# Second cross attention's first rows loaded by GpSimd, first experts' weights loaded a stage ahead

## The reference

```python
x = x + L0_attn(layernorm(x))                      # attention with a sigmoid/tanh/relu score
x = x + L0_xattn(layernorm(x), ctx, ctx)           # cross attention, 8 heads of 128
x = x + L0_ffn(layernorm(x))                       # 8 experts, top 2, width 1024
x = x + L1_attn(layernorm(x))
x = x + L1_xattn(layernorm(x), ctx, ctx, mask)     # cross attention, 16 heads of 16, below
x = x + L1_ffn(layernorm(x))                       # 64 experts, the best one
```

```python
# L0_ffn: routing, then the experts
logits = einsum('bsh,eh->bse', x, gate_w) + expert_bias
top_w, top_i = top_k(softmax(logits), 2)
for e in range(8):
    h = gelu(einsum('bsh,ih->bsi', x, w_up[e]), approximate=False)
    out += sparse_w[..., e:e + 1] * einsum('bsi,hi->bsh', h, w_down[e])
# L1_xattn
q, k, v = x @ Wq, ctx @ Wk, ctx @ Wv               # split into 16 heads of 16
A = softmax(q k^T / 4 - mask * 1e9)
x + (A v) @ Wo
```

## Time and profile before

| | |
|---|---|
| median of 3 runs | 2875.01 us (2874.33 to 2880.67) |
| profiled execution | 2879.26 us |
| its span | 2877.5 us |
| TensorE busy | 2514.8 us (87%) |
| VectorE busy | 2087.2 us (73%) |
| ScalarE busy | 1446.5 us (50%) |
| GpSimd busy | 1059.3 us (37%) |
| moved by DMA | 266.68 MB, mean 93 GB/s |

### The profile page before, as it was taken

One profiled execution on the slowest core, in us unless ns is written; L12 is line 12 of the kernel. 1 busy time (PEld: TensorE's weight loads), 2 busy tenths in 40 slices (PEclk: granted clock), 3 DMA queues, 4 the chain that ended last, 5 costly groups with the idle time before them and its releaser, 6 DMA issues. The chain is left out here.

```text
span 2877.5 us, 59452 instructions
## 1 busy us (share of the span) xinstructions
PE 2514.8 (87%) x19717; PEld 2098.5 (73%) x19717; DVE 2087.2 (73%) x4615; ACT 1446.5 (50%) x3401; POOL 1059.3 (37%) x1584
## 2 busy tenths in 40 slices
PE   7987899999758999999499999999996979996582
PEld 5875788888757999999378888888885956664231
DVE  5884898998637777776488888888875567774664
ACT  3542334334235777777265555655552456663041
POOL 3331545445301111110265555555532014333366
PEclk9988999999978999999699999999998989997586
DMA  8012000000176666664200000000002733230845
GB/s 310 0 32 88 1 1 0 0 0 0 31 292 249 220 220 220 220 219 156 90 14 10 16 7 15 7 15 9 7 1 65 246 102 87 81 88 11 267 142 168
DMA packets 156638, 266.68 MB, mean 93 GB/s; under 512 B 20944, under 2 KB 130464, under 8 KB 143200
## 3 DMA queue, kind: packets, MB, share of 16 engines
q1 hardware_dynamic: 140400, 215.91, 22.1%
q0 software_dynamic: 11168, 31.21, 3.7%
q10 hardware_dynamic: 4944, 17.96, 1.6%
HBM read 191.85 MB, written 73.17 MB: 92 GB/s over the span
## 5 line engine op out<-in xcount | busy, mean ns | idle before, releaser
L1723 ACT ACTIVATE a_prob<-a_s_ps,a_ntop 128x256 f32<-128x256 f32 x512 | 235.6, 473 | 304.3 <-DVE a_ntop L1808 304.3
L1776 POOL TENSOR_TENSOR a_prob<-a_prob,a_rden 128x1024 f32<-128x1024 f32 x128 | 242.5, 1895 | 302.4 <-DVE a_rden L1813 302.4
L3204 POOL DMA_INDIRECT e0x_xg<-token_rows,e_order x78 | 75.3, 965 | 384.7 <-PE e0x_t_ps L3251 342.5
L2411 ACT ACTIVATE x1a_prob<-x1a_st_ps,x1a_mask_now 128x512 f32<-128x512 f32 x256 | 162.2, 686 | 92.0 <-PE x1a_st_ps L2330 90.6
L1301 ACT ACTIVATE x0b_sq<-x0b_f 128x1024 f32<-128x1024 f32 x64 | 67.9, 1060 | 274.2 <-DVE x0b_f L1375 274.1
L2486 DVE TENSOR_REDUCE x1a_top<-x1a_s_ps 128x4 f32<-128x1024 f32 x128 | 154.9, 1222 | 66.9 <-PE x1a_s_ps L2314 65.0
L1808 DVE TENSOR_REDUCE a_ntop<-a_s_ps 128x4 f32<-128x1024 f32 x128 | 156.2, 1221 | 38.9 <-PE a_s_ps L1646 38.8
L68 PE MATMUL e0x_up_ps<-e0x_xT_high,e0x_up_w_high 128*128 128x256 f32 x624 | 180.4, 289 | 1.1 <-DVE e0x_up_w_low L3331 1.1
L68 PE MATMUL e0x_up_ps<-e0x_xT_high,e0x_up_w_low 128*128 128x256 f32 x624 | 177.5, 285 | 0.0
L68 PE MATMUL e0x_up_ps<-e0x_xT_low,e0x_up_w_high 128*128 128x256 f32 x624 | 177.3, 284 | 0.0
L68 PE MATMUL e0x_y_ps<-e0x_down_w_high,e0x_hT_high 128*128 128x256 f32 x624 | 176.6, 283 | 0.0
(11 more groups left out here) (648 smaller groups left out, 8708.1 us busy)
## 6 DMA issues: line engine op xcount, KB each, us to landing
e0x_up_raw<-up_rows SPq DMA_DIRECT2D x39, 1024.0 KB, 4.8
e0x_down_raw<-down_rows SPq DMA_DIRECT2D x39, 1024.0 KB
x_qk<-head_rows SPq DMA_DIRECT2D x384, 64.0 KB
head_rows<-x1p_rows_out SPq DMA_DIRECT2D x32, 512.0 KB, 3.8
e1w_ew<-in_L_ffn_expert_w_dram SPq DMA_DIRECT2D x8, 2048.0 KB
sorted_tokens<-zeros SPq DMA_DIRECT2D x10, 1024.0 KB, 19.6
sorted_results<-e0x_y SPq DMA_DIRECT2D x39, 256.0 KB
down_rows<-e0w_downT ACTq DMA_DIRECT2D x8, 1024.0 KB, 7.3
```

The costliest lines, as they stand in the source:

```text
L1723: last = act.activation(prob[:, h % RING, n, t, :], s_ps[:, n, t * SEQ:(t + 1) * SEQ], ACT.Exp, bias=ntop[:, h % RING, n, t:t + 1], accum_ ...
L1776: last = pool.tensor_tensor(p, p, scale_of, ALU.mult)
L2411: last = act.activation(prob[:, c % 2, j, 2 * (h % 2):2 * (h % 2) + 2, :], st_ps[:, :, j * SEQ:(j + 1) * SEQ], ACT.Exp, bias=mask_now[:, p ...
```

## The change

Two parts. In the first, a new class `Ahead` places the gate's weights and the first two copies of up and down matrices in SBUF at addresses that in the first cross attention belong to the context and the start of `wg` (so `wg` now comes before `out_bias`), and an SP block in `l0_cross_batches` loads them once the last F product is done. They have semaphores of their own, and the loads at the routing stage's start go. In the second, the 56 loads of batches 0 and 1 of the second cross attention are issued by GpSimd in the projections' block, as soon as that batch's stores are there, on semaphores `s_first`; SP issues from batch 2 on, and TensorE waits for `s_first` in batches 0 and 1.

```diff
-        self.out_bias = sb(cross, "x0_out_bias", [P, DIM])
         self.wg = [cross.enter_context(nc.sbuf_tensor(f"early_x0_wg_{part}", [P, KC, INNER], F32R)) for part in ("high", "low")]
+        self.out_bias = sb(cross, "x0_out_bias", [P, DIM])
...
         with nc.Block() as block:
+
+            @block.sync
+            def _(sp):
+                sp.wait_ge(filled["F"], COUNT["F"] * BATCH)
+                ahead.load(sp)
...
+        s_first = [[sem(f"rows{p}{half}_first") for half in range(2)] for p in range(2)]
...
+        def load(engine, b, p, half, landed):
+            i0 = slice(half * HALF, (half + 1) * HALF)
+            for n in range(2):
+                for side in range(2):
+                    for r, name in enumerate(ROWS_OF[side]):
+                        at = 64 * n + XROWS * r
+                        engine.dma_start(qk[p][at:at + XROWS, side, i0, :].bitcast(F32),
+                                         by_pair[PLANE[name], n][:, bass.ds(PAIRS * b + half * HALF, HALF), :]).then_inc(landed[p][half], 16)
+                at = 64 * n + 3 * XROWS
+                engine.dma_start(qk[p][at:at + 2, 1, i0, :].bitcast(F32),
+                                 head_rows.mask[:, bass.ds(b, 1), :].broadcast_to([2, HALF, SEQ])).then_inc(landed[p][half], 16)
...
                 pool.wait_ge(s_fixed, 7)
+                pool.wait_ge(s_rows, 32)
+                for b in range(2):
+                    pool.wait_ge(s_stored[b], 16 * KC)
+                    for half in range(2):
+                        load(pool, b, b, half, s_first)
...
-                for b in range(2):
-                    for half in range(2):
-                        load(b, b, half)
-
                 def batch(b, p):
                     for half in range(2):
                         sp.wait_ge(s_st, PAIRS * b + HALF * (half + 1))
-                        load(b + 2, p, half)
+                        load(sp, b + 2, p, half, s_ld)
...
                     if h % HALF == 0:
-                        pe.wait_ge(s_ld[p][h // HALF], 16 * LOADS * (turn + 1))
+                        if isinstance(turn, int) and turn == 0:
+                            pe.wait_ge(s_first[p][h // HALF], 16 * LOADS)
+                        else:
+                            pe.wait_ge(s_ld[p][h // HALF], 16 * LOADS * turn)
...
-                if given is None:
+                if given is None and ahead is None:
                     sp.dma_start(gw[:], gate_w).then_inc(s_w, 16)
                     sp.dma_start(gb[:], broadcast_row(gate_b)).then_inc(s_w, 16)
...
-                    pe.wait_ge(s_w, 32)
+                    pe.wait_ge(ahead.s_gate if ahead else s_w, 32)
...
             if n % 2 == 0:
-                pe.wait_ge(self.loaded[e % self.COPIES][n // 2], 16 * (e // self.COPIES + 1))
+                if self.first and e < self.COPIES:
+                    pe.wait_ge(self.first[e][n // 2], 16)
+                else:
+                    pe.wait_ge(self.loaded[e % self.COPIES][n // 2], 16 * (e // self.COPIES + (0 if self.first else 1)))
...
     def load(self, sp):
         first = TurnedWeights.COPIES
-        self.up.load(sp, 0, first)
-        self.down.load(sp, 0, first)
         self.up.load(sp, first)
         self.down.load(sp, first)
...
+class Ahead:
...
+    def load(self, sp):
+        sp.dma_start(self.gw[:], self.gate_w).then_inc(self.s_gate, 16)
+        sp.dma_start(self.gb[:], broadcast_row(self.gate_b)).then_inc(self.s_gate, 16)
+        self.up.load_ahead(sp, self.s_up)
+        self.down.load_ahead(sp, self.s_down)
```

More of the change, by code:

```diff
@@ L158, in __init__ @@
         self.c_rstd = sb(cross, "c_rstd", [P, TILES])
+        self.wg = [cross.enter_context(nc.sbuf_tensor(f"early_x0_wg_{part}", [P, KC, INNER], F32R)) for part in ("high", "low")]
         self.out_bias = sb(cross, "x0_out_bias", [P, DIM])
-        self.wg = [cross.enter_context(nc.sbuf_tensor(f"early_x0_wg_{part}", [P, KC, INNER], F32R)) for part in ("high", "low")]
         self.c1 = sb(cross, "x0_c1", [P, XH])
@@ L653, with l0_cross_attention @@
 INNER = XH * HD
-def l0_cross_attention(nc, sh, early, weights, w1, b1, g1, be1, w2, b2, w_up, up_rows):
+def l0_cross_attention(nc, sh, early, weights, w1, b1, g1, be1, w2, b2, w_up, up_rows, ahead):
     with ExitStack() as ctx:
@@ L2202, in _, with l1_cross_attend @@
                 over_batches(dve, batch)
-def l1_cross_attend(nc, sh, head_rows, gate, wo, v, sel, mask_col, qk, top_rows):
+def l1_cross_attend(nc, sh, head_rows, gate, wo, v, sel, mask_col, qk, top_rows, s_ld, s_first, load):
     HALF = PAIRS // 2
@@ L2560, in doubling_sum, with route @@
     return a
-def route(nc, sh, name, experts, top_k, tiles, gate_w, gate_b, slots, weights, table, chosen, beside=None, beside_out=None, beside_rows=None, load=None, granule=P, given=None, rows=None, found=None):
+def route(nc, sh, name, experts, top_k, tiles, gate_w, gate_b, slots, weights, table, chosen, beside=None, beside_out=None, beside_rows=None, load=None, granule=P, given=None, rows=None, found=None, ahead=None):
     E, K = experts, top_k
@@ L2571, in route @@
         sb, ps, sem = alloc(nc, ctx, name)
-        gw = sb("gw", [E, DIM])
+        gw, gb = (ahead.gw, ahead.gb) if ahead else (sb("gw", [E, DIM]), sb("gb", [P, E]))
         gwT = sb("gwT", [P, KC, E])
-        gb = sb("gb", [P, E])
         XN = 2 if rows is None else 4
@@ L2886, in __init__ @@
         self.experts = w.shape[0]
+        self.first = None
     def allocate(self, ps, sem):
@@ L2897, in signals, with load_ahead @@
         self.filled, self.drained = sem(f"{self.name}_in_psum"), sem(f"{self.name}_turned")
+    def load_ahead(self, sp, first):
+        self.first = first
+        for e in range(self.COPIES):
+            for half in range(2):
+                sp.dma_start(*self.half_of(e, half)).then_inc(first[e][half], 16)
     def load(self, sp, first=0, end=None):
@@ L3027, in dispatch_programs, with __init__, keep @@
     return vector, pool
+class Ahead:
+    TABLES = 248
+    def __init__(self, nc, sh, ctx, gate_w, gate_b, w_up, w_down):
+        E, I = w_up.shape[0], w_up.shape[1]
+        sem = lambda name: ctx.enter_context(nc.semaphore(f"ahead_{name}"))
+        self.gate_w, self.gate_b = gate_w, gate_b
+        self.s_gate = sem("gate_loaded")
+        self.s_up = [[sem(f"up{e}_half{half}_loaded") for half in range(2)] for e in range(TurnedWeights.COPIES)]
+        self.s_down = [[sem(f"down{e}_half{half}_loaded") for half in range(2)] for e in range(TurnedWeights.COPIES)]
+        with ExitStack() as space:
+            sb = lambda name, shape: space.enter_context(nc.sbuf_tensor(f"ahead_{name}", shape, F32))
+            sb("tables", [P, self.TABLES])
+            up_nat = sb("up_nat", [P, TurnedUp.COPIES, I // P, DIM])
+            down_nat = sb("down_nat", [P, TurnedDown.COPIES, KC, I])
+            self.gw = sb("gw", [E, DIM])
+            self.gb = sb("gb", [P, E])
+        self.words = TurnedUp.COPIES * I // P * DIM + TurnedDown.COPIES * KC * I + DIM + E
+        self.up = TurnedUp(sh, "up", w_up[AHEAD:E], up_nat, 2)
+        self.down = TurnedDown(sh, "down0", w_down[0:AHEAD], down_nat, 2)
+    def load(self, sp):
[3 more added lines that the diff above has]
+        self.down.load_ahead(sp, self.s_down)
+    def keep(self, nc, ctx):
+        ctx.enter_context(nc.sbuf_tensor("ahead_kept", [P, self.words], F32))
 class ExpertRows:
@@ L3052, in l0_experts @@
     with ExitStack() as ctx:
+        ahead.keep(nc, ctx)
         sb, ps, sem = alloc(nc, ctx, "e0w")
@@ L3060, in l0_experts @@
         down.signals(sem)
[L3061 to L3068, removed]
+        halves = TurnedHalves(ahead.up, ahead.down, rows_of.up[AHEAD * P:E * P, :], rows_of.down[0:AHEAD * P, :])
+        route(nc, sh, "e0r", E, K, NP, None, None, slots, weights, table, None, halves, (upT, downT[0]), (s_rows,),
+              load=lambda sp: down.load(sp, 0, TurnedDown.COPIES), granule=GROUP, rows=scratch.rows, ahead=ahead)
         with ExitStack() as invert:
```

33 lines of the change are left out of this document (12 added, 21 removed).

## The result

The changed kernel takes 2868.86 us at the median of 17 runs, the kernel before 2874.87 in 17 runs beside it: a ratio of 0.9976, 95% interval [0.9965, 0.9987]. So it is faster by about 0.24%: some 7 us by the ratio, 6.0 between the medians. The forecast was 27 us; 2868.86 lies above the top of its range. The profiled execution took 2867.18 us, 1.7 under its median, where that of before was 4.25 over the median of its first three runs.

A forecast was written before the change was run, and what follows sets the result against it. It took DMA waits in the routing stage and at the seam before the second cross attention as the bounds. Gains of 21 + 6 = 27 us gave 2852.3 profiled, 2848 for the median; range 2841 to 2862.

The forecast's parts named there:

- The gate's 2.9 us: Routing stage's start: TensorE begins with the block instead of waiting for the gate's weights, saving 2.9 us.
- The third pair, 12.2 us: Routing stage: the third pair, 17.21 us against the second's 4.98, gets its up weights earlier, saving 12.2 us.
- step (c): Routing stage's last pair: with 4.2 of 23 MB gone, less stands in front of its load, saving 7.4 us.
- I take 21, near the upper end: Routing stage: total gain taken as 21 us, between 13 and 22.5, since stores catch up while no load runs.
- The lower bound: Routing stage: loads at 105 GB/s throughout, up and down experts each 4.7 us late, leaving a gain of 13 us.
- rival 1: Routing stage stays bound by DMA: gain 13 + 6 = 19 us, time 2856; chance 0.17.
- The seam, 8.2 us: Between projections and second cross attention: first score 7.5 us sooner, 0.7 of the second wait; 8.2 together, at most 9.5.
- GpSimd's 56 issues in 30 us: Projections: GpSimd issues the 56 row loads in 30 us by the direct row, 53 by the indirect one.
- Rival 5: Slower: GpSimd's issues so slow that the attention waits for rows; at 2.5 us each, 12 slower, 2887; chance 0.04.
- The price in the projections, 2 us: Projections: row loads exceed the spare DMA room and delay context loads, costing 2 us of the seam's gain.
- rival 2: The projections pay the whole gain of the seam: gain 21 + 0, time 2854; chance 0.10.
- rival 4: Ahead loads land late or something else holds the pairs: only the seam's 6 us left, 2869; chance 0.03.

The follow-up runs named there:

- ahead_only: The changed kernel with the 56 row loads back on SP at the attention's start, weights still loaded ahead: 2865.14 us, ratio 0.9965 to the kernel before.
- stores_end: The changed kernel with all eight stores of turned expert weights issued behind the routing stage's last pair: 2856.89 us, ratio 0.9925 to the kernel before.
- pool_only: The kernel before with only the row loads issued by GpSimd, weights loaded as before: 2876.21 us, ratio 1.0003 to the kernel before.
- stores_late: The changed kernel with each routing-stage store of turned expert weights issued three pairs later: 2861.3 us, ratio 0.9954 to the kernel before.
- all_paced: The changed kernel with GpSimd's 56 row loads issued four at a time behind each of 14 stored batches: 2862.63 us, ratio 0.995 to the kernel before.
- first_paced: The changed kernel with GpSimd loading batch 0 alone, two loads behind each stored batch, SP loading batch 1 at the attention's start: 2860.11 us, ratio 0.9943.
- first_unpaced: The changed kernel with GpSimd loading batch 0 alone, 28 loads in one burst, SP loading batch 1 at the attention's start: 2871.91 us, a single run.
- e0r_t_ps: Not a run: a buffer in the routing stage that TensorE's matmuls write from ident and e0r_xn; no time of its own.
- e0r_xn: Not a run: the tile of VectorE's normalising in the routing stage, whose first operation marks the stage's start; no time of its own.
- e0r_up_ps: Not a run: a buffer in the routing stage that TensorE's matmuls write from ident and ahead_up_nat; no time of its own.

## Why the prediction was wrong

The direction was right (faster had 0.92), the size wasn't: 27 us were forecast, about 7 came. Step by step:

- **The loads ahead cost nothing**: right. They were issued from 735.56 to 741.9 and done by 750, in the empty stretch.
- **The gate's 2.9 us**: right. The stretch with that wait is 3.0 shorter.
- **The third pair, 12.2 us**: right to 0.1 by itself (17.21 to 4.98), but the fourth pair went from 4.99 to 12.24. **The last pair, 7.4**: in the change's profile 6.5 came (12.33 to 5.79), and the fifth and seventh gave back 0.8 and 1.5. The sum of the eight pairs fell by 9.5 us, 62.04 to 52.58, where 18.1 were taken. Even that was luck: in the four other kernels with these loads ahead and the stores in place the last pair took 12.54 to 13.35 us, so step (c), that less stands in front of its load, brought nothing in them.
- The step that failed here is the one behind "I take 21, near the upper end": that "the up loads start beside token rows alone, before the first expert's store". They were issued at 785.29 and the store followed at 787.29, so 18 of their 20 us lay beside stores, at 105 GB/s. The lower bound's working was the good one: it had these loads in at 807.2, and they were in at 805.3. Gate and stage together gave 12.5 in the change's profile, just under the bound of 13, and in the mean of the profiles 3.0 + 4.6 = 7.6; the runs of ahead_only have 10 us (the interval 7 to 13). This was rival 1, with a chance of 0.17: its mechanism was right, and its 13 the most that these loads may have brought. stores_end shows the mechanism: without stores beside the loads all such waits are gone and the stage is 10 us shorter.
- **The seam, 8.2 us**: right, 7.7, with the first score at its block's start; the attention behind it is 0.3 shorter, where 0.7 were taken for the second wait. Most of it was issue time. The row loads of the first score were issued one after the other by SP, from 2300.39 to 2306.48, 6.1 of the 7.75 us that the score waited:

```profile
2303.49 2.65 SPq L2285 DMA_DIRECT2D x_qk<-head_rows  x6
2306.19 0.29 SPq L2288 DMA_DIRECT2D x_qk<-mask_rows  x1
```

- **GpSimd's 56 issues in 30 us**: right, 0.514 us each by the direct row, all out by 2243.4, and no sign of VectorE holding them up (the longest took 0.647). Rival 5 had nothing behind it. It was also priced too low: these issues stand in the projections' block, and the attention's block begins only when they have ended, so issues until 2366 would have held up the block from 2300.4 on and not just the second batch's fifth score.
- **The price in the projections, 2 us**: the second step that failed. It was mis-sized beyond its own upper bound: 10.7 in the change and 7.6 in pool_only (9.3 and 8.9 in stores_late and stores_end), against 4.9 + 1.3 = 6.2. Three things were missing. The 11.2 us of engine time holds where the loads are spread out (11.1 in all_paced), not in a burst (14.4). Slack "of about 1" in the context loads was a guess; four context loads were late, by 1.07, 2.85, 0.17 and 2.58 us, and two stores were. And the granted clock fell behind those waits, which no term had: of the 10.5 us of missing matmuls, 6.7 us are TensorE's waits in that stretch, and the rest is what the lower clock took. This was rival 2, that the projections pay all that the seam gives, with 0.10.
- The page DMA: Bandwidth & Descriptors, section Issuing engines are not separate DMA queues, of the Trainium skill has it that loads share the same 16 DMA engines whichever engine starts them, and that starting them on several saves issue time alone. No run here goes against it: 6.1 us of the seam were issue time, and the loads, moved in a burst, cost the projections what the seam gave (pool_only, 1.0003). What the forecast had right beside it is that there was room at 0.83, but only over the whole stage: first_paced keeps 7.7 us at the seam and pays 0.5.
- The first two rivals were priced one at a time. Together they give 13 + 0, so 2879.26 - 13 = 2866.3 for the profiled execution, and it took 2867.18. They share one cause, full DMA engines, and so should have had one chance, with that case at the top of the range.
- In profiled times the change brought 12.1 us, in medians 6.0. The working was made against one profiled execution that was 4.25 above its median, the one after was below its own, and the waits for weights were larger before and smaller after than elsewhere. With means over the profiles the sum comes out: 7.6 for the weights' part, 8.0 for the seam and the attention, less 9.1 for the projections (10.7, 9.3, 8.9 and 7.6), is 6.5 us, as rough as its first term. That the time of 2868.86 is rival 4's 2869 is chance: that rival wanted ahead loads that land late, and they were there 30 us before the stage.

What stays open: why the routing stage with stores in place took 69.1 us in one profile and 79.0 in another. Waits for weights make the difference (5.5 us in all in first_paced, 11.7 in first_unpaced), but what sets which load falls behind was not tried. Nor was it tried whether holding back only some of the stores would do as well as all eight. The row loads in the projections came from GpSimd in every run; whether the same burst from SP's queue would cost the projections as much is not known, nor whether the first score's 14 loads, shared at the seam among several engines, would save most of the issue time without any load in the projections.

## What to carry to other kernels

A preload pays only if the transfers that stay behind it still meet their due times: take out the first of a row of loads and the wait goes to the next one, as long as stores fill the engines beside them. The cheaper repair is then to move the transfers that nobody waits for, here stores that could run a stage later. Where a stage leaves 17% of the DMA engines free, that room is there over the stage and not at once: issue extra loads a few at a time behind each step, and only the part that the next stage needs first. And a wait read from one profile is no price yet: here the same routing code took 69.1 to 79.0 us, and one pair of it 5.79 or 13.35.

## What the runs showed of the hardware

- Loads are served late beside stores. The change's four up loads of 512 KB in the routing stage landed 8.9 us after their issue at the median, with 392 GB/s moved in all (790 to 800 us); with the stores away, in stores_end, 4.4 us. For the last two it was 10.6 and 13.7 us against 4.3 and 6.0.
- A full DMA share is not one rate: 1.08 to 1.10 went with 273 to 311 GB/s in the projections, 1.04 with 425 GB/s where 1 MB stores ran in stores_end.
- A load of mask rows, 8 KB, took GpSimd 0.557 us to issue, a load of 64 KB 0.514: the issue did not grow with the size.
- The fourth pair's first transposes ran slower also where nothing had been waited for. In stores_end the first eight took 1.62 us and not 1.07, and the pair 6.2 us and not 5.0, with TensorE over 95% busy in the 10 us around it and a mean granted clock of 0.85 there:

```profile
796.58 1.62 PE L2671 MATMUL e0r_t_ps<-ident,e0r_xn 128*128 128x128 f32 x8
797.99 3.24 PE L2935 MATMUL e0r_up_ps<-ident,ahead_up_nat 128*128 128x128 f32 x16
```
